# Splitting the four row scatters of each batch into two pairs, in an adaLN block with windowed attention and a routed FFN

## The chip, the cores and the metric

The kernel runs on one core of one Trainium2 chip, as one launch. The metric is the device time of that launch in microseconds, as the median of several runs. Before the change it is 313.97 us (three runs: 309.85, 313.97, 314.17).

## What is computed

Eight batches of 256 tokens, 128 wide, go through one block: a modulated layer norm, attention over windows of 64 positions (each window sees itself and the one before it) with 16 heads of 8, a gated residual, a second modulated layer norm, and an FFN with eight experts of hidden width 352, of which each token takes two. All is fp32.

```python
mod = (_silu(L0_c) @ L0_wmod).reshape(L0_c.shape[0], 6, 1, -1)
sa, ca, ga, sb, cb, gb = (mod[:, 0], mod[:, 1], mod[:, 2], mod[:, 3], mod[:, 4], mod[:, 5])
ga = (2 * (ga >= 0) - 1) * jnp.maximum(jnp.abs(ga), 0.25)
gb = (2 * (gb >= 0) - 1) * jnp.maximum(jnp.abs(gb), 0.25)
h = _layernorm(x, axis=-1) * (1 + ca) + sa
x = x + ga * _L0_attn_ref(h, L0_attn_w_qkv, L0_attn_w_out)
h = _layernorm(x, axis=-1) * (1 + cb) + sb
x = x + gb * _L0_ffn_ref(h, L0_ffn_Wg, L0_ffn_W1, L0_ffn_W3, L0_ffn_W2)

# the FFN: the two best experts of each token, weighted by a softmax of their scores
scores = xt @ Wg.T
top_vals, top_idx = jax.lax.top_k(scores, TOPK)
weights = jax.nn.softmax(top_vals, axis=-1)
h1 = jnp.einsum('td,ehd->teh', xt, W1)
h3 = jnp.einsum('td,ehd->teh', xt, W3)
expert_out = jnp.einsum('teh,edh->ted', jax.nn.silu(h1) * h3, W2)
out = jnp.sum(sel * weights[:, :, None], axis=1)
```

## The kernel before

The program is written by hand for each engine; every engine runs its own list in order, and semaphores tie them. It has two stages.

**The attention stage** takes the batches b = 0 to 7 in turn. On TensorE (PE), ScalarE (ACT) and VectorE (DVE) a batch is `period0(b)` followed by `period1(b)`. The work is pipelined over batches: `period0(b)` of PE holds the scores of the second half of batch b (`scores`, L500, 64 small matmuls in the trace), the transpose of the second norm's result of batch b-2 (`h2_transpose`, L598), the projections Q and K of batch b+1 (`project_qk`, L463 and L464), the product with V of the half before (`pv(2b-1)`, L560, 64 small matmuls), the projection V (`project_v`, L469), the transposed scores (`scores_t`, L529 to L544), the gate of batch b-2 (L607), the output's transposition of batch b-1 (`output_t`, L575) and the transposed row maxima (`neg_max_t`, L510). `period1(b)` holds the same kinds of work for the other half, with `pv(2b)`. The product with V thus ends twice in a batch and counts the semaphore `pv_done` up by one each time.

DVE reduces the scores to row maxima (`neg_max`, L993, waits for `s_done`, which the last L500 counts up). ACT copies what PE leaves in PSUM (h2 transposed, L857; Q, L819; K, L820 and L821; the output, L844; V, L825) and takes the exponentials (L832, wait for `f_done`, which the last L544 counts up).

GpSimd (POOL) has the loop of this case. For each b it multiplies Q of batch b+1 by a mask into `qm` (`mask_q`, L1352, waits for `q_copied` and `f_done`; two buffers), inverts the standard deviation of batch b-1 (`inv_std2`, L1339, waits for DVE's variance in `period1(b)`), scatters the rows of batch b-2, and scales W_out (`gate_wout`, L1345).

**The scatters** put each token's second norm, twice (once for each chosen expert), with its token number, into the DRAM tensor `routed`, at the row that the token has in its expert's region. A batch has 256 tokens in two tiles of 128 (p = 0, 1) and two choices (k = 0, 1), so four indirect DMAs of 128 rows of 516 bytes (L1363). They read `pay[e % 2]` and `row_u[e % 2]`, and count up `scattered[e % 2]` as they land. DVE refills `pay[e % 2]` for batch e+2 in `modulate_2` only after that count (L1045).

**The FFN stage** takes slots of 128 rows of one expert. SP loads a slot's rows from `routed` (L408), PE transposes them (L732), multiplies by W1 and W3 (L720, L722), transposes the gated product (L736) and multiplies by W2 (L745); POOL scatters the results into `ranked` (`store`, L1406). The first twelve slots use rows of batches 0 to 4 alone, and start once these have landed and a first table is there. Batches 6 and 7 are scattered between the first stores. At the end each token's two rows are read back, weighted and added to x.

In the scheduling of the attention stage POOL's order is fixed by its list: what stands behind a waiting instruction waits too.

## Time and profile before

| | us |
|---|---|
| median of three runs | 313.97 |
| lowest, highest | 309.85, 314.17 |
| the profiled execution | 310.88 |
| its span in the trace | 309.0 |

The profile comes from one execution, whose own time is 310.88 us; 1.9 us of it lie around the span. Of the span PE is busy 234.9 us (76%), DVE 158.3 us (51%), ACT 115.0 us (37%) and POOL 109.4 us (35%). The attention stage lasts to about 175 us, the FFN slots run to about 286 us, and the rest is the final sum. Idle time of an engine matters only where its work ends last; so the chain from engine to engine within a batch is what is to be read.

### The profile page before, as it was taken

The page shows a single profiled execution, that of the slowest core. Times are in us where ns is not written, and L with a number is a line of the kernel's source. Part 1 is how long each engine was busy: PE and PEld are TensorE (multiplying, and loading weights), DVE is VectorE, ACT ScalarE, POOL GpSimd, SP SyncE. Part 2 cuts the span into 40 slices and gives each one's busy share as a digit, 9 for nine tenths or more (in the row PEclk, how much of TensorE's full clock was granted, in tenths as well). Part 3 has the DMA queues.
Part 4 walks back from the last instruction along what each step waited for, and adds up shares of the span by engine and source line. Part 5 has one row for each costly group of instructions (what it writes and reads, how often), then busy time and mean ns, then how long its engine had stood idle before and what let it go on. Part 6 is the DMA issues. An engine that isn't in the chain of part 4 may idle for free.

```text
span 309.0 us, 9635 instructions
## 1 busy us (share of the span) xinstructions
PE 234.9 (76%) x3654; PEld 173.3 (56%) x3655; DVE 158.3 (51%) x527; ACT 115.0 (37%) x259; POOL 109.4 (35%) x119
## 2 busy tenths in 40 slices
PE   7666898987979979797875799693099999997000
PEld 3445576766657657474553566472077877876000
DVE  2656669664934637365354254463034444443393
ACT  3214455544524424354043243131034444443250
POOL 8213132235070350624205107365023443435241
PEclk9959899999998979999579589798579999999755
DMA  5599000000010000100002002112112211210551
GB/s 132 152 405 430 10 2 4 2 14 28 2 37 4 11 28 2 40 2 20 19 2 56 15 17 61 46 52 67 53 44 60 59 44 54 54 45 29 169 192 57
DMA packets 16880, 19.46 MB, mean 63 GB/s; under 512 B 2962, under 2 KB 15382, under 8 KB 16586
## 3 DMA queue, kind: packets, MB, share of 16 engines
q1 hardware_dynamic: 14170, 14.44, 14.6%
q0 software_dynamic: 2240, 4.28, 4.2%
q8 instruction: 28, 0.46, 0.6%
q10 hardware_dynamic: 432, 0.20, 0.2%
q14 instruction: 10, 0.08, 0.1%
HBM read 13.04 MB, written 6.13 MB: 62 GB/s over the span
## 4 chain that ended last, share of the span: by engine, by line
PE 48%; issue 18%; DVE 8%; ACT 7%; DMA 5%; SPq 5%; another core or an unknown queue 4%; POOL 3%; DVEq 0%; POOLq 0%; ACTq 0%
PE pair L745 7%; PE pair L720 6%; PE pair L560 6%; PE pair L722 6%; ACT pt L832 4%; PE pair L736 3%; PE pair L534 3%; PE pair L500 3%; PE pair L575 2%; DVE fin_b L1311 2%; POOL qm L1352 2%; DMA x_all<-x 2%; PE pair L469 2%; DVE nd L993 2%
## 5 line engine op out<-in xcount | busy, mean ns | idle before, releaser
L1406 POOL DMA_INDIRECT ranked<-y_sb,ix_u x36 | 35.5, 987 | 54.3 <-ACT y_sb L918 42.4
L993 DVE TENSOR_REDUCE nd<-pair 128x8 f32<-128x1024 f32 x32 | 37.6, 1218 | 32.5 <-remote 19.4
L1287 DVE TENSOR_TENSOR gated<-pair,act 128x352 f32<-128x352 f32 x36 | 18.9, 524 | 47.6 <-PE pair L722 39.6
L832 ACT ACTIVATE pt<-pair 128x1024 f32<-128x1024 f32 x32 | 32.8, 1029 | 27.3 <-PE pair L544 27.3
L1339 POOL TENSOR_TENSOR rstd<-veps,cf_sb 128x2 f32<-128x2 f32 x8 | 6.0, 747 | 84.2 <-DVE veps L1033 84.2
L1363 POOL DMA_INDIRECT routed<-pay,row_u x32 | 31.8, 994 | 9.1 <-issue 9.1
L560 PE MATMUL pair<-pt,v_lane 128*32 128x64 f32 x1024 | 27.2, 241 | 8.4 <-issue 8.0
L745 PE MATMUL pair<-we_sb,gated_t 128*128 x216 | 31.6, 285 | 1.6 <-ACT y_sb L918 1.6
L720 PE MATMUL pair<-we_sb,x_t 128*128 x72 | 29.2, 489 | 2.3 <-issue 1.8
L745 PEld LDWEIGHTS pair<-we_sb,gated_t 128*128 128x128 f32 x216 | 28.3, 199 | 2.3 <-issue 2.3
L500 PE MATMUL pair<-k_sb,qm 32*64 32x128 f32 x1024 | 25.4, 291 | 5.3 <-POOL qm L1352 1.6
L560 PEld LDWEIGHTS pair<-pt,v_lane 128*32 128x32 f32 x1024 | 20.1, 122 | 16.5 <-issue 16.5
L722 PE MATMUL pair<-we_sb,x_t 128*128 x72 | 28.3, 476 | 0.0
L1300 DVE COPY gated_t<-pair 128x384 f32<-128x384 f32 x36 | 19.8, 550 | 10.7 <-PE pair L736 6.1
L500 PEld LDWEIGHTS pair<-k_sb,qm 32*64 32x64 f32 x1024 | 18.3, 136 | 10.3 <-issue 8.8
L907 ACT ACTIVATE act<-pair 128x352 f32<-128x352 f32 x36 | 16.7, 464 | 16.7 <-PE pair L720 12.1
L918 ACT COPY y_sb<-pair 128x128 f32<-128x128 f32 x36 | 9.6, 266 | 34.3 <-issue 14.6
L732 PE MATMUL pair<-cf_sb,xt_in 128*128 128x128 f32 x36 | 10.5, 293 | 12.4 <-DMA xt_in<-routed 9.3
L722 PEld LDWEIGHTS pair<-we_sb,x_t 128*128 128x128 f32 x72 | 14.3, 198 | 8.3 <-issue 1.2
L1352 POOL TENSOR_TENSOR qm<-q_sb,quadmask 128x1024 f32<-128x1024 f32 (+1 forms) x8 | 14.3, 1786 | 12.9 <-ACT q_sb L819 12.9
L534 PE MATMUL pair<-qm,k_sb 32*128 32x256 f32 x256 | 18.7, 409 | 0.0
L736 PE MATMUL pair<-cf_sb,gated 128*128 128x128 f32 x108 | 18.4, 281 | 0.0
(167 smaller groups left out, 390.1 us busy)
## 6 DMA issues: line engine op xcount, KB each, us to landing
we_sb<-we SPq DMA_DIRECT2D x1, 4352.0 KB, 18.3
xt_in<-routed SPq DMA_DIRECT2D x36, 64.5 KB
mod_bc<-mod_rows SPq DMA_DIRECT2D x1, 2048.0 KB, 8.2
fin_y<-ranked SPq DMA_DIRECT2D x8, 256.0 KB, 4.9
out<-fin_b SPq DMA_DIRECT2D x8, 128.0 KB, 1.8
x_all<-x SPq DMA_DIRECT2D x1, 896.0 KB, 5.5
ranked<-y_sb,ix_u POOLq DMA_INDIRECT x36, 2.3
routed<-pay,row_u POOLq DMA_INDIRECT x32
```

What stands on the lines that cost most here:

```text
L500: last = mm(S_BANKS[j][64 * a:64 * a + 64, quad * P:quad * P + P], group(qm[par], j)[:, quad, c * W:c * W + W], group(k_sb[par], j)[:, c * ...
L534: mm(fv[:, :, a * W:(a + 1) * W], group(k_sb[par], j)[:, c * W:c * W + 2 * W], group(qm[par], j)[:, :, c * W:(c + 1) * W], start=False, st ...
L560: last = mm(group(Z0, j)[:, at:at + W], v_lane[par][:, c * H + 4 * j + quad, low:low + 32], pt[:, j, quad * P + a * W:quad * P + a * W + W ...
L720: mm(H1_BANK[n][:, 0:HID], x_t[n][:, :], weights((r + 1) % 4, 0, HID), start=True, stop=True).then_inc(h1_done, 1)
L722: mm(H3_BANK[n][:, 0:HID], x_t[n][:, :], weights((r + 1) % 4, HID, HID), start=True, stop=True).then_inc(h3_done, 1)
L736: last = pe.transpose(GT_BANK[r % 2][:, k * P:(k + 1) * P], gated[r % 2][:, k * P:(k + 1) * P], ident)
L745: last = mm(Y_BANK[:, 0:D], gated_t[n][:, k * P:(k + 1) * P], weights((r - 1) % 4, 2 * HID + k * D, D), start=(k == 0), stop=(k == KT - 1))
L832: act.activation(pt[:, 2 * half:2 * half + 2, :].rearrange("p j k -> p (j k)"), src[:, :], ACT.Exp).then_inc(done, 1)
L993: dve.tensor_reduce(nd[:, :, 2 * half:2 * half + 2, 0].rearrange("p s j -> p j s"), src[:, :].rearrange("p (j s k) -> p j s k", j=2, s=4), ...
L1352: pool.tensor_tensor(qm[b % 2][:, 0:quads, :], q_sb[:, :].unsqueeze(1).to_broadcast([P, quads, S]), quadmask[:, 0:quads].unsqueeze(2).to_b ...
L1363: pool.indirect_dma_start(routed[:, :], at, pay[e % 2][:, p, k, :], None).then_inc(scattered[e % 2], 16)
L1406: pool.indirect_dma_start(ranked[:, :], bass.IndirectOffsetOnAxis(ap=ix_u[q][:, 0:1], axis=0), y_sb[q][:, :], None, bounds_check=TOPK * TO ...
```

## The change

POOL issues the four scatters of a batch in two pairs. The pair of tile 0 stays where all four were, in iteration b for batch b-2. The pair of tile 1 is issued in the next iteration, ahead of `mask_q`, and waits there for `pv_done` to reach 2b, which is the end of `pv(2b-1)` in `period0(b)`. For batch 5 it stands behind the loop and waits for the last product with V. Batches 6 and 7 are as they were.

```diff
-            def scatter(e):
-                rows_chosen(e)
-                for p in range(2):
-                    scatter_tile(e, p)
-
...
             for b in range(B):
+                if b >= 3:
+                    pool.wait_ge(pv_done, 2 * b)
+                    scatter_tile(b - 3, 1)
                 if b + 1 < B:
                     mask_q(b + 1, 4)
...
                 if b >= 1:
                     inv_std2(b - 1)
                 if b >= 2:
-                    scatter(b - 2)
+                    rows_chosen(b - 2)
+                    scatter_tile(b - 2, 0)
                 gate_wout(b)
+            pool.wait_ge(pv_done, G)
+            scatter_tile(B - 3, 1)
             inv_std2(B - 1)
```

On POOL, in the loop, at the place of the scatters of batch 0 (`pay0`) and batch 1 (`pay1`); `qm0` and `qm1` are the two mask buffers:

```order
-L1363 DMA routed<-pay0,row_u0 17536x129 x4
+L1363 DMA routed<-pay0,row_u0 17536x129 x2
 L1345 TENSOR_TENSOR wout_g<-wout_sb,mod_bc 128x128
+L1363 DMA routed<-pay0,row_u0 17536x129 x2
 L1352 TENSOR_TENSOR qm0<-q_sb,quadmask 128x1024
 L1339 TENSOR_TENSOR rstd2<-veps2,cf_sb 128x2
-L1363 DMA routed<-pay1,row_u1 17536x129 x4
+L1363 DMA routed<-pay1,row_u1 17536x129 x2
 L1345 TENSOR_TENSOR wout_g<-wout_sb,mod_bc 128x128
+L1363 DMA routed<-pay1,row_u1 17536x129 x2
 L1352 TENSOR_TENSOR qm1<-q_sb,quadmask 128x1024
```

Of each four, two now stand behind `gate_wout` and before the next mask, so that the mask has a wait for `pv_done` and two scatters ahead of it.

The same piece of POOL's list after the change, with what each instruction waits for:

```order
L1339 TENSOR_TENSOR rstd<-veps,cf_sb 128x2 [waits var2_ready]
L1363 DMA routed<-pay,row_u 17536x129 [waits pay_ready,rows_ready]
L1363 DMA routed<-pay,row_u 17536x129
L1345 TENSOR_TENSOR wout_g<-wout_sb,mod_bc 128x128 [waits y_done]
L1363 DMA routed<-pay,row_u 17536x129 [waits pv_done]
L1363 DMA routed<-pay,row_u 17536x129
L1352 TENSOR_TENSOR qm<-q_sb,quadmask 128x1024 [waits f_done,q_copied]
```

The wait for `pv_done` stands at the first scatter of the second pair alone.

On PE, where nothing moves, the list around that `pv` in `period0`:

```order
L500 MATMUL pair<-k_sb,qm 64x128 x32
L598 MATMUL pair<-cf_sb,pay 128x128 [waits h2_ready,exp_z]
L598 MATMUL pair<-cf_sb,pay 128x128
L463 MATMUL pair<-h_t,wqkv_sb 128x256 [waits ht_ready]
L464 MATMUL pair<-h_t,wqkv_sb 128x256
L560 MATMUL pair<-pt,v_lane 32x64 [waits v_copied,exp_z]
L560 MATMUL pair<-pt,v_lane 32x64 x31
L469 MATMUL pair<-wqkv_sb,h_t 128x128 [waits negt_ready]
L469 MATMUL pair<-wqkv_sb,h_t 128x128 x3
L529 MATMUL pair<-negt,cb_sb 128x512 [waits exp_z,o_copied,exp_x,h2t_copied,max_x,negt_ready]
```

The second pair is released when the last L560 has ended, so beside L469 and what follows it; the first pair is released by DVE and ACT, about when L500 runs. (An fp32 matmul stands once here and twice in the trace.)

## Rows read from the trace of the kernel before

**Rows 1.** Busy time by batch: start:end length, busy (instructions), PEclk, DMA share, GB/s.

```profile
50.49:65.65 15.16, 14.15 (x407) 10.93 (x407) 11.95 (x38) 8.60 (x17) 3.05 (x3) 1.00 0.02 4
65.65:84.19 18.54, 15.79 (x407) 11.64 (x407) 11.05 (x38) 8.56 (x17) 7.16 (x7) 1.00 0.05 17
84.19:104.34 20.15, 17.51 (x407) 12.88 (x407) 10.62 (x38) 8.39 (x17) 7.12 (x7) 0.92 0.05 16
104.34:124.52 20.18, 17.58 (x407) 12.90 (x406) 10.61 (x38) 8.36 (x17) 7.12 (x7) 0.92 0.05 16
124.52:142.54 18.02, 15.71 (x389) 11.41 (x389) 10.78 (x36) 7.77 (x16) 7.12 (x7) 1.00 0.06 18
142.54:164.77 22.23, 17.76 (x294) 11.99 (x294) 10.12 (x47) 6.21 (x11) 5.23 (x7) 0.69 0.05 15
164.77:186.13 21.36, 15.62 (x125) 10.72 (x122) 7.77 (x39) 7.71 (x16) 5.22 (x6) 0.76 0.13 32
```

**Rows 2.** Timeline of POOL, batch 2's scatters: start, us, engine line [idle before].

```profile
104.34 0.76 POOL L1339 TENSOR_TENSOR rstd<-veps,cf_sb 128x2 f32<-128x2 f32 x1 [10.86 <-DVE veps L1033]
105.30 1.12 POOL L1363 DMA_INDIRECT routed<-pay,row_u  x1 [0.20 <-issue]
...
109.25 0.96 POOL L1363 DMA_INDIRECT routed<-pay,row_u  x1 [0.30 <-issue]
...
111.72 1.89 POOL L1352 TENSOR_TENSOR qm<-q_sb,quadmask 128x1024 f32<-128x1024 f32 x1 [1.02 <-ACT q_sb L819]
```

**Rows 3.** Timeline of PE, DVE and ACT beside and behind those scatters.

```profile
107.62 0.72 PE L560 MATMUL pair<-pt,v_lane 128*32 128x64 f32 x10
...
108.74 0.34 PE L560 MATMUL pair<-pt,v_lane 128*32 128x64 f32 x6 [0.40 <-issue]
...
110.95 2.36 DVE L993 TENSOR_REDUCE nd<-pair 128x8 f32<-128x1024 f32 x2 [5.20 <-remote]
110.96 0.81 PE L560 MATMUL pair<-pt,v_lane 128*32 128x64 f32 x39 [0.44 <-issue]
110.99 0.37 ACT L857 COPY h_t<-pair 128x256 f32<-128x256 f32 x1 [4.93 <-remote]
...
111.70 1.98 PE L469 MATMUL pair<-wqkv_sb,h_t 128*128 128x128 f32 x8
...
116.16 1.02 ACT L832 ACTIVATE pt<-pair 128x1024 f32<-128x1024 f32 x1 [1.86 <-PE pair L544]
```

**Rows 4.** The same timeline a stage earlier, in a batch without scatters.

```profile
51.98 2.34 DVE L993 TENSOR_REDUCE nd<-pair 128x8 f32<-128x1024 f32 x2
...
54.44 1.16 PE L469 MATMUL pair<-wqkv_sb,h_t 128*128 128x128 f32 x8
...
57.29 1.02 ACT L832 ACTIVATE pt<-pair 128x1024 f32<-128x1024 f32 x1 [1.07 <-PE pair L544]
...
59.14 1.21 PE L500 MATMUL pair<-k_sb,qm 32*64 32x128 f32 x64
```

**Rows 5.** Timeline of PE and ACT beside batch 5's scatters (165.72 to 170.63).

```profile
167.41 1.30 PE L560 MATMUL pair<-pt,v_lane 128*32 128x64 f32 x45
167.52 0.37 ACT L857 COPY h_t<-pair 128x256 f32<-128x256 f32 x1 [0.70 <-PE pair L598]
```

**Rows 6.** Timeline: last of seven indirect DMAs in a row, and PE behind it.

```profile
211.80 0.99 POOL L1406 DMA_INDIRECT ranked<-y_sb,ix_u  x1 [0.31 <-issue]
...
212.86 0.85 PE L720 MATMUL pair<-we_sb,x_t 128*128 x2 [1.82 <-issue]
```

**Rows 7.** Stretches of 2 us behind those scatters: PE busy (instructions), PEclk, DMA share.

```profile
110.00:112.00 2.00, 1.34 (x45) 0.96 0.10 33
112.00:114.00 2.00, 2.00 (x12) 0.50 0.04 8
```

**Rows 8.** Timeline of PE and ACT in batch 7's first half, behind batch 4's scatters.

```profile
150.39 1.94 PE L560 MATMUL pair<-pt,v_lane 128*32 128x64 f32 x64
...
156.08 1.02 ACT L832 ACTIVATE pt<-pair 128x1024 f32<-128x1024 f32 x1 [3.31 <-PE pair L544]
```

## The prediction, made before the changed kernel ran

> **What bounds the kernel now.** I read the busy time by batch first. Six stretches, each from one `inv_std2` (L1339) to the next, differ in one thing: the first, 50.49 to 65.65, has no scatter and takes 15.16 us; the next four have four scatters each and take 18.54, 20.15, 20.18 and 18.02 us, with (but for the last) the same 407 matmuls. POOL's busy time grows by 4 us in them, yet POOL is busy only 7 of 18 to 20 us, so POOL isn't the bound. Two more stretches, 142.54 and 164.77, take 22.23 and 21.36 us [rows 1]. What do the scatters do to the others?
>
> The timeline answers. POOL issues the scatters of batch 2 from 105.30 to 109.25 + 0.96 = 110.21 [rows 2]. Beside them, PE starts `pv` at 107.62, does 10 of its 64 matmuls, and then goes on in small groups: 6 at 108.74, two more groups like it, and the last 39 at once from 110.96. DVE's `neg_max`, which waits for nothing but the end of L500, is idle for 5.20 us and starts at 110.95; ACT's copy L857, which waits for the transpose on PE, is idle for 4.93 us and starts at 110.99 [rows 3]. Three engines come free together, 0.74 us behind the last scatter. So while scatters are generated, PE's signals reach others late, and PE itself stops once some tens of its instructions are out. Batch 5's scatters show the second part alone: PE comes to them idle, ACT gets its signal after 0.70 us, 45 of the 64 matmuls go out at full speed, and only then does PE stop [rows 5]. I call this state the slow phase. It ends with the burst: also behind a burst of seven in the FFN stage, whose last ends at 211.80 + 0.99 = 212.79, and PE goes on at 212.86 [rows 6]. So it ends 0.1 to 0.7 us behind the last indirect DMA.
>
> The chain of a batch runs through it: `pv`, then L469, then the transposed scores, then the exponentials (L832, "pt"). Without scatters L469 starts at 54.44, 3.95 us into the stretch, and pt at 57.29, 6.80 in [rows 4]. With them L469 starts at 111.70, 7.36 in, and pt at 116.16, 11.82 in [rows 3]. From pt to the next L1339 both take the same: 65.65 - 57.29 = 8.36 and 124.52 - 116.16 = 8.36. All that a stretch loses, it loses before pt.
>
> A part of the loss is the clock. In the stretches of 20.15 and 20.18 us the granted clock is 0.92 in the mean, in those of 18.54 and 18.02 it is 1.00 [rows 1]: behind the slow phase, in which PE does little, it falls to 0.50, the lower level (1.2 GHz), for about 3 us [rows 7]. L469 then takes 1.98 us instead of 1.16 [rows 3, 4]. The price is 20.15 - 18.54 = 1.6 us.
>
> **The change, part by part.**
>
> *First pair stays.* A scatter costs POOL 0.96 + 0.30 = 1.26 us [rows 2]. With two fewer, the burst ends 2.52 us earlier, at 107.69, and the slow phase at 108.43 instead of 110.95. DVE and ACT start 2.5 us earlier. PE has 54 of the 64 matmuls left; 39 took until L469 starts 0.74 us later [rows 3], so 54 take 1.0: L469 at 109.4, 5.1 us into the stretch, and the wait for `pv_done` is over at the same time.
>
> *Second pair.* POOL starts it 0.20 later and needs 1.12 + 0.30 + 0.96 = 2.38 us [rows 2]: 109.6 to 112.0. This makes a second slow phase, until 112.7. PE does L469 and the transposed scores in it, 32 matmuls (8, 4, 16, 4) before the last group, against the 128 of L500 and `pv` in the old one. By the row of 45 matmuls [rows 5] PE has room for that many without a stop, so PE is not stopped; but the signal for the exponentials is behind in the queue and comes with the end of the phase. By PE's own pace pt would start 57.29 - 54.44 = 2.85 us behind L469 [rows 4], at 112.25; by the slow phase at 112.7 to 112.8. I take 112.8, that is 8.4 us into the stretch. The bounds: 7.95 (PE's own pace), and 9.2 if the phase ends 0.7 us later.
>
> *A stretch* is then 8.4 + 8.36 = 16.8 us. Against 18.54 and 18.02 I take 1.7 us each (18.02 has 18 matmuls fewer, so its new length is shorter too), against 20.15 and 20.18 3.4 each, because the poor stretch of PE falls from over 5 us to about 2.5 and I expect the clock to hold. Together 10.2 us. If the clock falls as before, 3.2 less.
>
> *Stretch 142.54.* Here `pv` starts at 150.39, takes 1.94 us at half clock, and pt starts at 156.08 [rows 8]. Its start moves 2.5 earlier, to 147.9; its end is 149.0 to 149.8 by the clock; plus 0.2 + 2.38 + 0.74 gives pt at 152.3 to 153.1. That is 3.0 to 3.8 earlier; I take 3.5.
>
> *Stretch 164.77.* 45 matmuls go out by 168.7 [rows 5], beside which the first pair would end at 168.1. The remaining 19 took four groups of five, some 0.74 us apart (110.96 less two such steps in rows 3), 2.9 us; now 0.4. The second pair (batch 5, behind the loop) lies beside the gate and `output_t`, 12 matmuls. The clock may return earlier. I take 3.0 (bounds 1.5 and 4.5).
>
> *The wait and what it holds.* Behind the waiting scatter stand the mask (L1352), `inv_std2` and the first pair of the next batch. The mask ran from 111.72 for 1.89 us [rows 2]; it now runs from about 112.1 to 114.0. L500 of the next half needs it, 59.14 - 57.29 = 1.85 us behind pt [rows 4], so at 114.6, with 0.6 us to spare. The cover is thin: if pt starts at 112.25, L500 is due at 114.1 and little is left. I put 0.2 us a stretch on it, 1.0 in all. `inv_std2` isn't due before the end of the stretch. DVE refills `pay` only at the start of the next stretch, over 8 us behind the second pair. SP's first loads need batch 4's second pair, issued before pt of batch 7's first half; the table that they also need is written in `period1(7)`, later. All these cost nothing.
>
> *Sum.* 10.2 + 3.5 + 3.0 - 1.0 = 15.7 us. The profiled execution takes 310.88, so 295.2. The median of the three runs lies 3.1 above that execution and its lowest run 1.0 below; I add half of 3.1, since part of such scatter between runs may be the clock behind these phases: 296.7.
>
> **The rivals.**
>
> *The second burst gives most of it back (16 in 100).* The phase ends 0.7 us later than I took, and the clock falls as in rows 7. A stretch is 9.2 + 8.36 + 1.6 = 19.2, against a mean of (18.54 + 20.15 + 20.18 + 18.02) / 4 = 19.2: four stretches gain nothing, the last two some 4: about 307 to 309. For it: two phases have two beginnings and two ends. Against: the second lies beside a quarter of the matmuls.
>
> *Nothing changes (7 in 100).* The late signals have another cause, and the scatters merely lie beside it. Then it stays at 311 to 314. Against it: six bursts with the same picture, and a stretch without any [rows 1, 4].
> The Trainium skill's page "SBUF — State Buffer", section "Who interferes with whom", speaks for this rival: only VectorE and GpSimd share a port pair, and TensorE and ScalarE never wait on anyone. By it a scatter being generated couldn't hold PE, and the change would be worth 0 instead of 15.7 us. Rows 3 disagree, with PE stopped and ACT 4.93 us idle, though the cause need not be a port of SBUF.
>
> *Slower: the slow phase has a fixed length (5 in 100).* It lasted 110.95 - 105.30 = 5.65 us. If two scatters make as long a phase as four, L469 stays at 7.36 us in, the second phase ends at 7.36 + 0.2 + 5.65 = 13.2, and pt with it, against 11.8 (half clock) and 18.54 - 8.36 = 10.2 (full clock). Two stretches lose 1.4, two 3.0, the last two perhaps 1 each: 310.9 + 10.8 = 322. It decides once a pair's phase is longer than some 4.5 us. Against it: the ends of rows 3 and 6 follow the last DMA, after four and after seven.
>
> **How the numbers follow.** The forecast has 72 in 100, with its own range 289 (PE's own pace, upper bounds of the last two) to 303 (the clock falls, lower bounds). With half of the first rival the range reaches 306. This kernel's measurement can tell about 2%, 6.3 us of 313.97, from no change. All of the forecast and half of the first rival lie under 307.7: faster 0.80. The other half and "nothing changes": 0.15. Slower: 0.05.
>
> **What would show it.** In the new trace each of the four stretches should take about 17 us with a clock of 1.00; DVE's L993 should start 0 to 0.8 us behind the second scatter's end, its wait down from 5.2 to about 2.7; L469 should start about 5 us in; the second pair should start 0.2 us behind `pv`, and pt 0.7 behind its end. The mask should end before L500 is due, with a PE wait for POOL under 0.3. Wrong would be: `pv` still in small groups behind the pair's end; a pt later than 9.2 in; a clock of 0.5 behind either pair; a PE wait for `qm` of a microsecond.

## The result, and the profile after

The changed kernel takes 291.53 us in the median of 4 runs (289.18 to 293.05), the kernel before 312.34 on the same chip (4 runs, 309.85 to 314.17). The ratio is 0.933, with a 95% interval of 0.923 to 0.944: faster by 6.7%. The forecast was 296.7 (289 to 306). The profiled execution takes 289.18 us, 21.7 less than that of before; its granted clock is 0.894 in the mean, against 0.874. Here and below a ratio leaves out runs at a lower clock that took over 1.5% longer than the fastest of their kernel, while medians and ranges count every run.

The busy time by batch, from one `inv_std2` (L1339) to the next; columns as in rows 1 (start:end, length, then busy time and instructions of PE, PEld, DVE, ACT and POOL, granted clock, DMA share, GB/s):

```profile
50.53:65.70 15.17, 14.15 (x407) 10.95 (x407) 11.96 (x38) 8.59 (x17) 3.05 (x3) 1.00 0.02 4
65.70:81.62 15.92, 14.79 (x407) 11.22 (x407) 10.50 (x38) 8.38 (x17) 7.21 (x8) 1.00 0.06 20
81.62:97.47 15.85, 14.93 (x407) 11.21 (x406) 10.51 (x38) 8.38 (x17) 7.17 (x8) 1.00 0.06 20
97.47:113.34 15.87, 14.93 (x407) 11.20 (x405) 10.49 (x38) 8.37 (x17) 7.17 (x8) 1.00 0.06 20
113.34:128.71 15.37, 14.86 (x389) 10.98 (x388) 9.98 (x36) 7.61 (x16) 7.16 (x7) 1.00 0.07 21
128.71:146.95 18.24, 14.10 (x294) 10.00 (x294) 10.02 (x47) 7.16 (x12) 5.26 (x6) 0.81 0.06 18
146.95:164.40 17.45, 13.91 (x121) 9.77 (x122) 7.77 (x39) 6.92 (x16) 5.24 (x7) 0.80 0.15 39
```

The stretch without scatters is what it was (15.17 us). The six with scatters are 2.6, 4.3, 4.3, 2.6, 4.0 and 3.9 us shorter than in [rows 1], 21.8 together: the whole difference of the two executions lies here, and nothing is given back in the FFN stage behind it. POOL is as busy as before, 7.2 us in a stretch. The clock is 1.00 in the four middle stretches, where two of them had 0.92.

What a stretch looks like now. This is the timeline of PE, its weight loads (PEld), DVE, ACT and POOL in the stretch from 97.47; columns: start, us, engine, line, operation, out<-in, and in brackets the idle time before it:

```profile
99.85 0.96 POOL L1363 DMA_INDIRECT routed<-pay,row_u  x1 [0.30 <-issue]
...
100.75 1.45 PE L560 MATMUL pair<-pt,v_lane 128*32 128x64 f32 x64
...
101.14 0.89 PEld L560 LDWEIGHTS pair<-pt,v_lane 128*32 128x32 f32 x57 [0.25 <-issue]
101.32 2.36 DVE L993 TENSOR_REDUCE nd<-pair 128x8 f32<-128x1024 f32 x2 [2.44 <-remote]
101.36 0.37 ACT L857 COPY h_t<-pair 128x256 f32<-128x256 f32 x1 [2.18 <-remote]
...
102.12 1.16 PE L469 MATMUL pair<-wqkv_sb,h_t 128*128 128x128 f32 x8
...
102.47 1.01 POOL L1363 DMA_INDIRECT routed<-pay,row_u  x1 [1.18 <-PE pair L560]
...
103.79 0.96 POOL L1363 DMA_INDIRECT routed<-pay,row_u  x1 [0.30 <-issue]
...
104.63 0.29 PE L544 MATMUL pair<-cb_sb,late 32*32 32x256 bf16 x4
...
104.77 1.90 POOL L1352 TENSOR_TENSOR qm<-q_sb,quadmask 128x1024 f32<-128x1024 f32 x1
...
105.32 1.09 PE L575 MATMUL pair<-perm_o,o_sb 128*128 128x72 f32 x8
105.32 1.02 ACT L832 ACTIVATE pt<-pair 128x1024 f32<-128x1024 f32 x1 [1.42 <-PE pair L544]
...
106.45 0.36 DVE L1007 RECIPROCAL rden<-pair 128x32 f32<-128x32 f32 x1 [2.31 <-PE pair L575]
...
106.82 1.21 PE L500 MATMUL pair<-k_sb,qm 32*64 32x128 f32 x64
```

The first pair ends at 99.85 + 0.96 = 100.81. DVE and ACT start 0.51 and 0.55 us later, both out of a wait put down to "remote": the mark of the slow phase is still there, but the wait is 2.44 us instead of 5.20 [rows 3]. `pv` is no longer cut into small groups: its 64 matmuls are one row of 1.45 us, and only their weight loads pause once, for 0.25 us after the seventh. (Without scatters `pv` takes 1.10 us.) The second pair starts 0.27 us behind them and ends at 104.75, and the exponentials (`pt`) start at 105.32, 7.85 us into the stretch; before it was 11.82 [rows 3], without scatters 6.80 [rows 4]. The mask ends at 106.67 and L500 starts at 106.82, 9.35 us in (8.65 without scatters [rows 4]).

One subtraction sorts the rest. L469 starts 4.65 us in, against 3.95 without scatters [rows 4]: 0.70 late. The stretch is 15.87 us long, against 15.17: 0.70 as well. So in this stretch all that the scatters still cost is the first pair's; the second costs nothing.

### The profile page after: what moved, and what is told of

It is laid out like the page before. It is cut to its first block, busy times and chain, and to the rows that moved or that the text cites. A ratio compares the mean times of both kernels' runs of the same rounds, so it can differ in the third digit from the quotient of the medians.

```text
span 287.3 us, 9635 instructions
## 1 busy us (share of the span) xinstructions
PE 223.6 (78%) x3654; PEld 165.8 (58%) x3655; DVE 157.2 (55%) x527; ACT 114.8 (40%) x259; POOL 109.4 (38%) x119
## 4 chain that ended last, share of the span: by engine, by line
PE 51%; issue 16%; DVE 10%; POOL 8%; ACT 5%; DMA 4%; another core or an unknown queue 2%; ACTq 1%; SPq 1%; POOLq 0%; DVEq 0%
PE pair L745 8%; PE pair L720 8%; PE pair L722 7%; PE pair L560 4%; PE pair L736 4%; PE pair L500 3%; ACT pt L832 3%; POOL routed L1363 3%; POOL qm L1352 3%; PE pair L534 3%; DVE fin_b L1311 2%; PE pair L575 2%; PE pair L732 2%; DVE nd L993 2%
## 5 line engine op out<-in xcount | busy, mean ns | idle before, releaser
L993 DVE TENSOR_REDUCE nd<-pair 128x8 f32<-128x1024 f32 x32 | 37.7, 1220 | 19.1 <-remote 9.8
L1363 POOL DMA_INDIRECT routed<-pay,row_u x32 | 32.1, 1003 | 16.8 <-PE pair L560 9.5
L720 PE MATMUL pair<-we_sb,x_t 128*128 x72 | 30.3, 505 | 3.7 <-ACT x_t L912 3.7
L745 PE MATMUL pair<-we_sb,gated_t 128*128 x216 | 31.0, 280 | 1.7 <-ACT y_sb L918 1.7
L722 PE MATMUL pair<-we_sb,x_t 128*128 x72 | 29.2, 488 | 0.0
L745 PEld LDWEIGHTS pair<-we_sb,gated_t 128*128 128x128 f32 x216 | 27.7, 196 | 2.3 <-issue 2.3
L1339 POOL TENSOR_TENSOR rstd<-veps,cf_sb 128x2 f32<-128x2 f32 x8 | 6.0, 744 | 58.2 <-DVE veps L1033 58.2
L500 PE MATMUL pair<-k_sb,qm 32*64 32x128 f32 x1024 | 24.0, 292 | 3.6 <-DVE qm L1168 1.5
L500 PEld LDWEIGHTS pair<-k_sb,qm 32*64 32x64 f32 x1024 | 17.8, 137 | 7.8 <-issue 6.1
L918 ACT COPY y_sb<-pair 128x128 f32<-128x128 f32 x36 | 9.6, 266 | 31.1 <-issue 15.9
L560 PE MATMUL pair<-pt,v_lane 128*32 128x64 f32 x1024 | 20.7, 232 | 0.3
L560 PEld LDWEIGHTS pair<-pt,v_lane 128*32 128x32 f32 x1024 | 17.2, 117 | 5.1 <-issue 5.0
L912 ACT COPY x_t<-pair 128x128 f32<-128x128 f32 x36 | 9.6, 266 | 21.8 <-PE pair L732 17.0
L534 PE MATMUL pair<-qm,k_sb 32*128 32x256 f32 x256 | 17.2, 381 | 0.0
```

The lines of the kernel that those rows point to most:

```text
L500: last = mm(S_BANKS[j][64 * a:64 * a + 64, quad * P:quad * P + P], group(qm[par], j)[:, quad, c * W:c * W + W], group(k_sb[par], j)[:, c * ...
L534: mm(fv[:, :, a * W:(a + 1) * W], group(k_sb[par], j)[:, c * W:c * W + 2 * W], group(qm[par], j)[:, :, c * W:(c + 1) * W], start=False, st ...
L560: last = mm(group(Z0, j)[:, at:at + W], v_lane[par][:, c * H + 4 * j + quad, low:low + 32], pt[:, j, quad * P + a * W:quad * P + a * W + W ...
L720: mm(H1_BANK[n][:, 0:HID], x_t[n][:, :], weights((r + 1) % 4, 0, HID), start=True, stop=True).then_inc(h1_done, 1)
L722: mm(H3_BANK[n][:, 0:HID], x_t[n][:, :], weights((r + 1) % 4, HID, HID), start=True, stop=True).then_inc(h3_done, 1)
L745: last = mm(Y_BANK[:, 0:D], gated_t[n][:, k * P:(k + 1) * P], weights((r - 1) % 4, 2 * HID + k * D, D), start=(k == 0), stop=(k == KT - 1))
```

## Experiments

All times are medians; where a ratio has an interval, it is against the kernel before on the same chip. "Stretches" are the six lengths that follow the stretch without scatters, in the order of the profile. Each diff shows the part that matters, with ` ...` where lines are left out. Where lines are added ahead of them, a kernel's line numbers are a little higher than those of the kernel before; the text says which is which.

### The split without the hold

```diff
             for b in range(B):
                 if b >= 3:
-                    pool.wait_ge(pv_done, 2 * b)
                     scatter_tile(b - 3, 1)
 ...
-            pool.wait_ge(pv_done, G)
             scatter_tile(B - 3, 1)
```

> The four scatters stay split in two pairs in POOL's list, but the second pair no longer waits for the end of the product with V; only gate_wout (0.47 us) lies between the pairs. Theory 'place' (the loss comes from how many PE instructions stand beside the scatters while they are generated): POOL runs one burst of some 5.4 us again, beside L500 and pv, DVE's L993 waits about 5 us, and each of the four full stretches from one inv_std2 to the next takes 18 to 20.5 us instead of 15.9; the time is that of the kernel before, 308 to 316 us. Rival 'split' (two short bursts are milder than one long one, wherever they are): the gap ends the slow phase, stretches of 16 to 17 us, time 290 to 298 us.

Measured: 312.55 us (10 runs, 309.57 to 314.59), ratio 0.995 [0.991, 1.000]. Stretches 18.65, 20.13, 20.22, 19.67, 22.35 and 21.38. One stretch of it, by busy time as above:

```profile
84.68:104.81 20.13, 17.26 (x407) 12.84 (x407) 11.53 (x38) 8.57 (x17) 7.19 (x8) 0.92 0.05 16
```

POOL's timeline in it shows that only `gate_wout` (L1345) now stands between the two pairs:

```profile
87.07 0.96 POOL L1363 DMA_INDIRECT routed<-pay,row_u  x1 [0.30 <-issue]
88.05 0.47 POOL L1345 TENSOR_TENSOR wout_g<-wout_sb,mod_bc 128x128 f32<-128x128 f32 x1
88.68 1.01 POOL L1363 DMA_INDIRECT routed<-pay,row_u  x1 [0.17 <-issue]
```

What DVE and PE do beside and behind them:

```profile
89.33 2.36 DVE L993 TENSOR_REDUCE nd<-pair 128x8 f32<-128x1024 f32 x2 [3.23 <-remote]
...
91.56 1.07 PE L560 MATMUL pair<-pt,v_lane 128*32 128x64 f32 x27 [0.42 <-issue]
```

The stretch has the old length, but it isn't the old picture. I had expected DVE's L993 to wait for 5 us; it waits for 3.23, and in the four full stretches for 2.57, 3.23, 3.23 and 2.52, about 2 less than with four in a row (4.54, 5.21, 5.20 and 4.48). With the gap of 0.65 us DVE's signal comes through 1.30 us behind the first pair's end and with the third scatter still running. PE doesn't come free: `pv` goes on in small groups, and its last 27 matmuls start at 91.56, 0.60 us behind the last scatter's end (90.96). So what makes the stretch long is that PE is stopped at `pv`; the early signal to DVE gains nothing by itself.

The medians, 312.55 and 312.89, differ by 0.1%, and the ratio leaves at most 1%: the program order alone can't be told from no change. The gain is in the wait for `pv_done`, that is, in where the second pair runs.

### All four held

```diff
                 if b >= 3:
                     pool.wait_ge(pv_done, 2 * b)
+                    rows_chosen(b - 3)
+                    scatter_tile(b - 3, 0)
                     scatter_tile(b - 3, 1)
 ...
-                if b >= 2:
-                    rows_chosen(b - 2)
-                    scatter_tile(b - 2, 0)
                 gate_wout(b)
             pool.wait_ge(pv_done, G)
+            rows_chosen(B - 3)
+            scatter_tile(B - 3, 0)
             scatter_tile(B - 3, 1)
```

> All four scatters of a batch are held until pv in period0 has ended, none is left beside L500. Theory 'place': the first half of the stretch runs as in one without scatters, L469 starts about 4.0 us in; the burst then lies from 4.2 to 9.1 us in, the signal for the exponentials comes with its end, pt at about 9.7 instead of 7.85, so a stretch takes 9.7 + 8.36 = 18.1 us; the time is about 299 to 303 us. Rival 'only dense matmuls matter' (behind pv the scatters cost nothing, since PE has few instructions there): pt at 7 to 7.3, stretches of 15.3 to 15.7 us, if not for the mask, which ends 11 us in, where L500 is due 9 in; with that wait about 17, time 293 to 296 us and a PE wait for qm of 1 to 2 us.

Measured: 304.7 us (4 runs, 303.34 to 305.9), ratio 0.973 [0.968, 0.978]. Stretches 17.74, 19.28, 19.81, 19.07, 17.25 and 19.82. The second of them:

```profile
81.98:101.26 19.28, 16.07 (x396) 12.13 (x392) 10.79 (x38) 8.56 (x16) 7.04 (x8) 0.91 0.05 17
```

Its timeline (ACT, DVE, PE):

```profile
91.52 1.02 ACT L832 ACTIVATE pt<-pair 128x1024 f32<-128x1024 f32 x1 [2.21 <-PE pair L544]
...
93.75 0.36 DVE L1007 RECIPROCAL rden<-pair 128x32 f32<-128x32 f32 x1 [6.25 <-remote]
...
94.83 1.20 PE L500 MATMUL pair<-k_sb,qm 32*64 32x128 f32 x64 [1.91 <-POOL qm L1352]
```

`pt` starts 91.52 - 81.98 = 9.54 us in, as expected (9.7). The total was missed by both expectations: the median lies 1.7 us above the range of the theory (299 to 303), and the rival had the PE wait for `qm` right (1 to 2 us) but not the times. Two things make this stretch longer than the 18.1 expected. DVE's L1007, which waits for L575, starts only 0.99 us behind the burst's end (92.76), 11.77 us into the stretch; without scatters it is 58.77 - 50.49 = 8.28. From L1007 to the next L1339 it takes 6.9 us where nothing comes between (shown under "Second pair" below), which makes 18.65. The other 0.6 us come with the mask, for which PE waits 1.91 us, and with the clock (0.91 in this stretch, 0.83 in the third). The place behind `pv` is better than the old one even for four, but a burst there has limits of its own: the next signals that are due, and POOL's next product.

### No scatters at all, and the same bytes by direct DMAs

The batches' scatters (batches 0 to 5) are left out of the kernel before; `routed` is filled once with the padding row by SP so that the FFN stage has what to read. This fill moves everything behind it 8.4 us later, so only lengths are compared.

```diff
                 if b >= 1:
                     inv_std2(b - 1)
-                if b >= 2:
-                    scatter(b - 2)
                 gate_wout(b)
```

> The kernel before without the scatters of batches 0 to 5 (their rows never reach the experts; routed and ranked are filled with padding rows by SP after the weights instead, so that the slots have something to read). Theory 'the scatters are the whole difference': each of the four full stretches takes 15.2 us as the one without scatters does, PEclk 1.00, and the last two lose 5 us or more each; span 278 to 284 us. Rival 'the scatters merely lie beside it': stretches stay at 18 to 20 us, span near 309.

Measured: 293.27 us, one run (the kernel before beside it: 313.91, one run). Stretches 15.16, 15.17, 15.23, 14.62, 14.08 and 19.72. By busy time:

```profile
74.08:89.24 15.16, 14.12 (x407) 10.90 (x405) 11.94 (x38) 8.56 (x17) 3.05 (x4) 1.00 0.01 3
...
148.34:168.06 19.72, 16.08 (x121) 11.50 (x122) 7.96 (x39) 6.92 (x16) 1.15 (x3) 0.65 0.09 21
```

From the first to the last row of these six it is 93.98 us, against 120.48 before and 98.70 after. By that the scatters cost 26.5 us and 4.7 are left, but the last stretch spoils the sum: at a clock of 0.65 it takes 19.72 us without any scatter near, more than the changed kernel's 17.45. That can't come from slow phases; it comes back below. The first five alone take 74.26 us here, 99.12 before and 81.25 after: the scatters cost 24.9 there, and 7.0 of it are left. The span, 291.4 us, is over the 278 to 284 expected, by less than the fill's 8.4 us; and the last stretch lost 1.6 us where 5 or more had been expected.

In the next kernel each batch's four blocks of `pay` go to a scratch area by four direct DMAs of the same size, issued by SP, with their completion counted; the rows aren't scattered.

```diff
 ...
+                for p in range(2):
+                    for k in range(TOPK):
+                        at = (4 * e + 2 * p + k) * P
+                        sp.dma_start(aside_rows[at:at + P, :], pay[e % 2][:, p, k, :]).then_inc(direct[e % 2], 16)
```

> The kernel before with POOL's four scatters of each of batches 0 to 5 replaced by four direct DMAs of the same 128 x 516 bytes from SP's queue into another DRAM tensor (the rows never reach the experts; padding rows are filled in instead). The same bytes leave in rows of the same size at the same point of the stretch. Theory 'generation on POOL': no slow phase, DVE's L993 starts as without scatters, stretches of 15.2 to 15.5 us, span 278 to 284. Rival 'traffic': the rows on their way to DRAM, or their completion signals, hold PE's signals; stretches of 17 to 20 us, span over 295.

Measured: 291.4 us, one run. Stretches 15.17, 15.15, 15.23, 14.62, 14.08 and 19.58; the second one:

```profile
87.99:103.14 15.15, 14.11 (x407) 10.90 (x407) 11.94 (x38) 8.56 (x17) 3.05 (x3) 1.00 0.08 21
```

The same to 0.14 us as with no scatters, though the DMA share rises from 0.01 to 0.08. So the same bytes in direct DMAs of SP, with their completion signals, make no slow phase. (The span, 289.5 us, is again over the range, with a fill and a last stretch as in the kernel without scatters.)

### The same four DMAs from POOL, direct instead of indirect

Again the blocks go to the scratch area and the rows aren't scattered; the rows are written one behind the other.

```diff
                 for p in range(2):
                     for k in range(TOPK):
-                        at = bass.IndirectOffsetOnAxis(ap=row_u[e % 2][:, 2 * p + k:2 * p + k + 1], axis=0)
-                        pool.indirect_dma_start(routed[:, :], at, pay[e % 2][:, p, k, :], None).then_inc(scattered[e % 2], 16)
+                        at = (4 * e + 2 * p + k) * P
+                        pool.dma_start(aside_rows[at:at + P, :], pay[e % 2][:, p, k, :]).then_inc(scattered[e % 2], 16)
```

> The kernel before with the four scatters of each of batches 0 to 5 replaced by four direct DMAs of the same 128 x 516 bytes from POOL's own queue into another DRAM tensor (the rows never reach the experts; padding rows are filled in instead). In the profile such a DMA takes POOL about 0.7 us instead of 0.96. Theory 'generation on POOL, whatever its kind': a shorter burst (about 3.5 us with the gaps), a slow phase of 4 to 4.5 us, stretches of 16.5 to 18.5 us, span 288 to 300. Rival 'only the indirect form does it': stretches of 15.2 us, span 278 to 284.

Measured: 287.21 us, one run. Stretches 15.08, 15.08, 15.14, 14.50, 14.61 and 15.54. By busy time:

```profile
87.69:102.77 15.08, 14.20 (x407) 10.94 (x405) 11.83 (x38) 8.56 (x17) 5.28 (x8) 1.00 0.07 21
...
147.02:162.56 15.54, 11.12 (x125) 8.14 (x122) 7.79 (x39) 7.60 (x16) 3.39 (x7) 1.00 0.20 44
```

And POOL and DVE in the timeline (L1004 is what is L993 in the kernel before):

```profile
88.40 2.20 POOL L1381 DMA_DIRECT2D aside_rows<-pay  x4
...
89.10 2.36 DVE L1004 TENSOR_REDUCE nd<-pair 128x8 f32<-128x1024 f32 x2
```

This struck down my theory that any DMA that POOL issues makes the slow phase: it expected 16.5 to 18.5 us a stretch. POOL works 2.20 us on four direct ones, at the place and from the buffers of the old scatters, and PE doesn't notice. Nor is it that 2.20 us are too short to be felt: a pair of indirect ones takes POOL 2.38 us at this place and makes DVE wait for 2.44, while here DVE starts L1004 with no wait, beside POOL's work. It is the indirect form that does it. What the targets add, rows spread over `routed` against rows in order, wasn't tested by itself.

### Half the rows in each scatter

The scatters stay where they were, but each writes 64 rows instead of 128; the other half of the routed rows is left out.

```diff
-                        at = bass.IndirectOffsetOnAxis(ap=row_u[e % 2][:, 2 * p + k:2 * p + k + 1], axis=0)
-                        pool.indirect_dma_start(routed[:, :], at, pay[e % 2][:, p, k, :], None).then_inc(scattered[e % 2], 16)
+                        at = bass.IndirectOffsetOnAxis(ap=row_u[e % 2][0:W, 2 * p + k:2 * p + k + 1], axis=0)
+                        pool.indirect_dma_start(routed[:, :], at, pay[e % 2][0:W, p, k, :], None).then_inc(scattered[e % 2], 16)
```

> The kernel before with each of the four scatters of batches 0 to 5 cut to its first 64 rows (the other rows never reach the experts; padding rows are filled in by SP after the weights). Theory 'the slow phase is the making of the indirect descriptors, row by row': a scatter takes POOL 0.5 to 0.7 us instead of 0.96, the burst about 3.5 us instead of 4.9, and the stretches are 16 to 17.5 us. Rival 'a fixed cost of the indirect form': the same 0.96 us and stretches of 18 to 20 us. A third outcome: the same time on POOL but a shorter or no slow phase, which would tie the slow phase to the rows and not to POOL's busy time.

Measured: 317.73 us, one run (before: 310.81), with a start that the fill moves later. Stretches 18.54, 20.21, 20.12, 19.67, 20.87 and 21.36, in all 120.8 us against 120.5 before. By busy time:

```profile
89.79:110.00 20.21, 17.17 (x407) 12.79 (x407) 10.63 (x38) 8.47 (x17) 6.83 (x7) 0.92 0.04 9
```

And from the timeline of the next stretch:

```profile
114.70 0.90 POOL L1381 DMA_INDIRECT routed<-pay,row_u  x1 [0.30 <-issue]
...
116.64 0.37 ACT L867 COPY h_t<-pair 128x256 f32<-128x256 f32 x1 [4.92 <-remote]
```

(L867 is what is L857 in the kernel before, and L1381 are the scatters.) Half the rows (9 GB/s instead of 16) save POOL 0.06 us of 0.96 and PE nothing; ACT idles 4.92 us as before. The theory that the price is paid row by row fell, and the fixed cost held: between 64 and 128 rows the price goes with the number of indirect DMAs, not with rows or bytes. The burst ends at 114.70 + 0.90 = 115.60 and ACT comes free 1.04 us later, where it was 0.78 before [rows 2, 3].

### The mask ahead of the second pair

```diff
             for b in range(B):
+                if b + 1 < B:
+                    mask_q(b + 1, 4)
                 if b >= 3:
                     pool.wait_ge(pv_done, 2 * b)
                     scatter_tile(b - 3, 1)
-                if b + 1 < B:
-                    mask_q(b + 1, 4)
```

> As the changed kernel, but POOL writes the mask for the next batch ahead of the wait and the second pair, so the pair starts about 6.7 us into the stretch instead of 5.0. Theory 'signals are queued': the pair then lies beside the transposed scores' last matmuls and their signal, which comes with the end of the pair, 9.1 + 0.5 = 9.6 us in, and beside the next L500; pt at 9.0 to 9.6, stretches of 17.3 to 18 us, time 297 to 301 us. Rival 'the end of pv alone matters': any place behind pv is as good, and the mask is no longer near PE's need: stretches of 15.5 to 15.9, time 288 to 292 us.

Measured: 295.83 us (4 runs, 294.3 to 298.14), ratio 0.942 [0.936, 0.947]. Stretches 16.51, 16.56, 16.52, 16.07, 20.80 and 20.03. Busy time and timeline of the second:

```profile
82.81:99.37 16.56, 15.01 (x407) 11.32 (x406) 10.63 (x38) 8.37 (x17) 7.14 (x8) 1.00 0.06 19
```

```profile
90.74 1.09 PE L575 MATMUL pair<-perm_o,o_sb 128*128 128x72 f32 x8
90.89 0.96 POOL L1363 DMA_INDIRECT routed<-pay,row_u  x1 [0.30 <-issue]
90.94 1.02 ACT L832 ACTIVATE pt<-pair 128x1024 f32<-128x1024 f32 x1 [1.62 <-PE pair L544]
...
92.47 0.36 DVE L1007 RECIPROCAL rden<-pair 128x32 f32<-128x32 f32 x1 [2.78 <-PE pair L575]
```

A stretch takes 16.5 us instead of 15.9: neither the 17.3 to 18 of the theory that the pair's end rules `pt`, nor no cost at all. `pt` starts 8.13 us in, 0.91 ahead of the pair's end (91.85), so that signal came through. But the one behind it did not: DVE's `rden` (L1007) waits for L575 and starts 1.73 us behind that line's start and 0.62 behind the pair's end, where in the changed kernel it starts 1.13 behind L575 (105.32 to 106.45). 0.60 us late here, 0.6 us longer the stretch. From L1007 to the end of the stretch it is 6.90 us, as everywhere. So a pair costs by the signal that is due when it ends; moving it 1.8 us later (6.8 us in, not 5.0) made it meet another one. The time, 295.83 us, is between the two expectations as well, but only 2.6 us of it are these four stretches: the fifth takes 20.80 us at a clock of 0.61 and the sixth 20.03 at 0.73, though no mask is moved in them. The changed kernel has 18.24 and 17.45 there, and 17.72 and 19.56 in a second profile. Why isn't known.

### Each pair behind a `pv`

```diff
                 if b >= 3:
                     pool.wait_ge(pv_done, 2 * b)
-                    scatter_tile(b - 3, 1)
+                    rows_chosen(b - 3)
+                    scatter_tile(b - 3, 0)
                 if b + 1 < B:
                     mask_q(b + 1, 4)
+                if b >= 3:
+                    pool.wait_ge(pv_done, 2 * b + 1)
+                    scatter_tile(b - 3, 1)
```

(The pair of tile 0 at its old place is gone, and behind the loop the last batch's four follow the last `pv`.)

> Both pairs are held: the first until pv in period0 has ended, the second until pv in period1 has ended, each with a burst of its own behind a pv; nothing is left beside L500. Theory 'place': the first pair ends 6.6 us in, pt at 7.15 instead of 7.85 (0.7 us less a stretch), and the second pair delays the second exponentials by about as much (phase end 14.7 us in, instead of 14.0): stretches of 15.7 to 16.1, time 288 to 293 us, as the changed kernel. Rival 'what is left of the loss lies all in the first pair beside L500': stretches of 15.2 to 15.4 us, time 284 to 288 us. A third outcome: the rows land too late for DVE's refill of pay (L1046), which then waits, and a stretch takes 16.3 or more.

Measured: 289.41 us (4 runs, 288.01 to 290.99), ratio 0.924 [0.918, 0.931]. Stretches 15.17, 16.19, 15.84, 15.34, 15.80 and 19.27. By busy time:

```profile
65.75:80.92 15.17, 14.10 (x391) 10.85 (x390) 10.59 (x38) 7.77 (x16) 7.11 (x7) 1.00 0.07 21
```

From its timeline:

```profile
72.99 1.03 ACT L832 ACTIVATE pt<-pair 128x1024 f32<-128x1024 f32 x1 [1.51 <-PE pair L544]
...
80.55 1.02 ACT L832 ACTIVATE pt<-pair 128x1024 f32<-128x1024 f32 x1 [2.52 <-PE pair L544]
```

With one pair behind the first `pv` (70.10 to 72.48) and nothing at the old place, `pt` starts 7.24 us in, 0.44 later than without scatters, and the stretch still takes 15.17 us, as without: a pair in this place costs nothing. The second pair, which POOL issues from 77.59 to 79.87, holds up the second exponentials in the same way (idle 2.52 us), and its price shows in the next stretch, 15.8 us or so. In the middle stretches two pairs behind two `pv` cost as much as the changed kernel's two places. The gain is in the stretch from 128 (15.80 against 18.24): there the first pair at its old place still caught L500.

One thing could have spoiled the comparison: the pair behind the second `pv` lands late, and DVE waits for it before it refills `pay` (waits: total us, count, longest):

```profile
DVE pay L1046 <- DMA routed<-pay,row_u: 2.8, 2, 2.3
```

The two waits lie in the last two stretches, before the refills at 130.99 (2.27 us) and 145.08 (0.56).

A third buffer of `pay`, and of `row_u` and the count that goes with it, takes that wait away; in that kernel batch 5's scatters are placed as in the changed kernel.

```diff
-        pay = [sb(f"pay{i}", [P, 2, TOPK, PAY]) for i in range(2)]
+        pay = [sb(f"pay{i}", [P, 2, TOPK, PAY]) for i in range(3)]
 ...
```

> As the run with both pairs behind a pv, with a third buffer for pay and row_u, so that DVE's refill no longer waits for the second pair to land, and with batch 5's pairs as in the changed kernel. Theory 'signals': what that run still loses (0.7 us a stretch) is the second pair's slow phase in front of the second exponentials; the third buffer changes it by 0.2 us at most, stretches of 15.6 to 15.9 us, time 286 to 290. Rival 'landing': the refill's wait for the rows to land was the loss; stretches of 15.2 us, time 283 to 286.

Measured: 287.39 us (4 runs, 286.54 to 288.32), ratio 0.928 [0.922, 0.933]. Stretches 15.18, 15.86, 15.79, 15.28, 14.48 and 19.48.

The first four stretches don't move by more than 0.33 us, as the theory had it: in them the late signal is the cost, not the landing. The stretch from 128 becomes 1.3 us shorter, though this kernel differs there in the buffers and in batch 5's place at once, so that gain isn't divided between them.

### One, two and one

```diff
                 if b >= 3:
                     pool.wait_ge(pv_done, 2 * b)
-                    scatter_tile(b - 3, 1)
+                    scatter_tile(b - 3, 0, (1,))
+                    scatter_tile(b - 3, 1, (0,))
                 if b + 1 < B:
                     mask_q(b + 1, 4)
+                if b >= 3:
+                    pool.wait_ge(pv_done, 2 * b + 1)
+                    scatter_tile(b - 3, 1, (1,))
 ...
-                    scatter_tile(b - 2, 0)
+                    scatter_tile(b - 2, 0, (0,))
```

> The four scatters of a batch go out as one, two and one: the first where all four were (behind inv_std2, beside L500), the next two behind pv of period0 as the changed kernel's second pair, the last behind pv of period1. Batch 5's last three stand behind the last pv. Theory 'place and length': a single scatter's slow phase (1.0 us and 0.5) ends before anything on the chain needs a signal. Beside L500 it releases L993 about 2.6 us into the stretch, where L529 needs its result only at 5.1; behind the second pv it ends 13.3 us in, before f_done at 13.7. So the 0.7 us a stretch that the changed kernel still loses goes: stretches of 15.2 to 15.4 us instead of 15.87, time 282 to 286 us, 2 to 2.5% under the changed kernel's. Rival 'each burst costs its own beginning and end': three bursts cost more than two, stretches of 16.2 or more, time 291 to 295.

Measured: 287.84 us (4 runs, 283.53 to 288.92), ratio 0.921 [0.910, 0.932]. Stretches 15.71, 15.31, 15.52, 14.90, 14.92 and 19.58. DVE in the timeline of the third of them, which starts at 96.16:

```profile
98.62 2.36 DVE L993 TENSOR_REDUCE nd<-pair 128x8 f32<-128x1024 f32 x2 [1.06 <-PE pair L500]
```

With a single scatter at the old place DVE's wait is 1.06 us, where a pair makes 2.44 and four made 5.20, and L993 starts 2.46 us into the stretch. The first four stretches are 0.1 to 0.6 us above those without scatters, the fifth 0.8. So the theory was right that a single scatter is the mildest and the rival (16.2 or more) fell, but 15.2 to 15.4 us wasn't reached throughout, and the time is above the 282 to 286 expected; the last stretch, 19.58 us, is as long as in the two kernels beside it.

The changed kernel ran once more in the same comparison:

> The changed kernel once more, beside the other orders on the same chip: 289 to 293 us, four stretches of 15.4 to 15.9 us.

Measured: 292.71 us (4 runs, 291.71 to 293.33), ratio 0.944 [0.939, 0.950]. Stretches 15.91, 15.87, 15.85, 15.35, 17.72 and 19.56; the last by busy time:

```profile
146.17:165.73 19.56, 15.38 (x133) 10.94 (x130) 7.78 (x39) 7.71 (x16) 5.25 (x7) 0.74 0.13 35
```

The middle four repeat to 0.02 us; the last one took 17.45 us at a clock of 0.80 in the first profile and takes 19.56 at 0.74 here. On this chip "one, two and one" is 292.71 - 287.84 = 4.9 us below the changed kernel, 1.7%, and the kernel with three buffers 5.3 us. No run of either reaches into those of the changed kernel beside them (at most 288.92 against at least 291.71). Between the two of them the times don't decide. Against the kernel before these three comparisons are less firm: its seven runs on this chip go from 308.59 to 368.00 us.

## Why the prediction was right, point by point

The direction and the mechanism held, the time came 5 us under the forecast. The working was 15.7 us of saving on the profiled execution; it is 21.7. In the four middle stretches 13.9 us were saved, more than even the better bound of the working allows (10.2 and four times 0.45, 12.0): the range held because it was wide, not because each term was.

**What bounds the kernel: right, and now shown.** The reading was that scatters being issued on POOL hold up PE and its signals. Without scatters the stretches with 18.0 to 20.2 us take 14.6 to 15.2; with the same bytes from SP too. The reading lacked one word, "indirect": direct DMAs on POOL do nothing of the kind. And it took the late signals and the stop of PE for one thing: without the hold DVE's signal came 2 us earlier and the stretch stayed as long, so at the old place the stop of PE is what costs. "Nothing changes" is out with that. That rival had the Trainium skill's page "SBUF — State Buffer", section "Who interferes with whom", behind it, by which TensorE and ScalarE never wait on anyone. The runs disagree for whatever it is that indirect DMAs do: ACT is idle for 4.93 us ahead of its copy L857 [rows 3], and for 0.27 us in the kernel whose POOL sends the same bytes from the same buffers by direct DMAs. They don't say that it is a port of SBUF.

**The end of the slow phase: right.** DVE and ACT start 0.51 and 0.55 us behind the first pair's end (0 to 0.8 was named), DVE's wait is 2.44 us (about 2.7).

**First pair, a term sized too small.** I had PE free again 0.74 us behind the pair's end, with 54 matmuls left that take 1.0 us, and L469 at 5.1 us in. The 1.0 us was right: 57 weight loads are left, and from them (101.14) to L469 (102.12) it is 0.98. What was mis-sized is the end of the phase for PE: 101.14 - 100.81 = 0.33 us behind the pair's end, not 0.74. `pv` has hardly begun to be held by then, and L469 starts 102.12 - 97.47 = 4.65 us in, 0.45 better.

**Second pair, the other one.** I took `pt` at 8.4 (bounds 7.95 and 9.2); it is 7.85. From L469 to `pt` it takes 3.20 us, against 2.85 without scatters [rows 4]: the pair makes the signal only 0.35 us late. That signal comes 0.57 us behind the pair's end, as the text had it (0.7 to 0.8). The step that failed is the next one: "a stretch is then 8.4 + 8.36", all that is lost before `pt` is lost for good. From `pt` to the next L1339 it takes 113.34 - 105.32 = 8.02 us, 0.34 less than the 8.36 carried over. What the end of the stretch hangs on is not `pt` but DVE's L1007, which waits for L575 and not for the exponentials. These are its rows in the kernel before, in the stretch without scatters and in one with four:

```profile
56.95 0.29 PE L544 MATMUL pair<-cb_sb,late 32*32 32x256 bf16 x4
...
58.77 0.36 DVE L1007 RECIPROCAL rden<-pair 128x32 f32<-128x32 f32 x1 [2.62 <-PE pair L575]
...
117.64 0.36 DVE L1007 RECIPROCAL rden<-pair 128x32 f32<-128x32 f32 x1 [3.75 <-PE pair L575]
```

From L1007 to the next L1339 it takes 6.88 us (58.77 to 65.65), 6.88 (117.64 to 124.52) and 6.89 in the changed kernel (106.45 to 113.34), whether `pt` is late or not. L500 too starts 2.19 us behind L544 in both (104.63 to 106.82; 56.95 to 59.14 without scatters). The 8.36 was the same in both rows of before because `pt` started 0.34 us behind L544 in each, which a pair beside it changes. By my working the part from L469 to the end of the stretch is 16.8 - 5.1 = 11.7 us; it is 15.87 - 4.65 = 11.22, and 15.16 - 3.95 = 11.21 without scatters [rows 1, 4]. A delay of `pt` by 0.35 us is swallowed whole. Together the four stretches save 13.9 us for a forecast of 10.2.

**The clock in the four stretches: right.** It stays at 1.00.

**The last two stretches: nearly right, in part by luck.** Saved are 4.0 (forecast 3.5) and 3.9 (forecast 3.0, bounds 1.5 and 4.5). In the second profile of the changed kernel it is 4.5 and 1.8, so how close the two sizes came is a matter of the execution; the clock is 0.80 in the last stretch of one and 0.74 in that of the other. In the first of the two stretches the first pair still catches L500 and then the clock falls, as this timeline of PE and ACT in the changed kernel shows:

```profile
129.64 0.99 PE L500 MATMUL pair<-k_sb,qm 32*64 32x128 f32 x33
130.91 2.58 PE L500 MATMUL pair<-k_sb,qm 32*64 32x128 f32 x31 [0.28 <-issue]
...
134.05 1.94 PE L560 MATMUL pair<-pt,v_lane 128*32 128x64 f32 x64
...
139.06 1.02 ACT L832 ACTIVATE pt<-pair 128x1024 f32<-128x1024 f32 x1 [2.64 <-PE pair L544]
```

33 matmuls go out at speed, the other 31 take 2.58 us, and `pv` behind them takes 1.94, as in [rows 8]. So "`pv` starts 2.5 earlier at half clock" held as it was put (5.34 us in, against 7.85), and `pt` is 3.2 us earlier (10.35 us in, against 13.54), inside the 3.0 to 3.8.

**The mask: right on the mechanism, priced too high.** I put 1.0 us on it. It ends 0.15 us before L500 starts, L500 starts 2.19 us behind L544 as without scatters, and PE has no wait for `qm`. The cover is as thin as the text said: with two scatters more (all four held) PE waits 1.91 us.

**The sum.** 13.9 + 4.0 + 3.9 is 21.8, against 10.2 + 3.5 + 3.0 - 1.0: of the 6.1 us missed, 3.7 lie in the two sizes above (0.45 and 0.48 in each of four stretches), 1.4 in the last stretches, 1.0 in the mask. The 1.5 us added for the median was 2.35. "The second burst gives it back" and "a fixed length" fell: one scatter makes 1.06 us of DVE's wait, two 2.44, four 5.20, and without scatters there is none.

**What stays open.** Which part of an indirect DMA on POOL does it, and by what path it reaches PE, wasn't separated; that 64 rows cost nearly what 128 do speaks for something fixed in each. And why the clock falls in the last stretch (0.65 with no scatters, 1.00 with direct DMAs from POOL, 0.80 and 0.74 in two profiles of the changed kernel) isn't explained; it is worth up to 4 us (19.72 against 15.54), so single profiles can't rank kernels that differ by less there. For the same reason the 1.7% of "one, two and one" rests on its runs alone, whose spread is 5.4 us, and not on stretches of one profile.

## What to carry to other kernels

When several engines come out of waits put down to "remote" at one moment, and PE runs in small groups just before, look for what POOL did until then; indirect DMAs cost other engines more than POOL's own time. Place them where PE has few matmuls to issue and no signal that another engine needs next, in bursts of one or two, and look at what POOL owes next, since that cover is thin. A short gap in a burst isn't enough: it let DVE's signal through here and still kept PE in small groups. Where the rows are known beforehand, the direct form costs nothing here, from SP or from POOL.

## What the runs showed of the hardware

- An indirect DMA of 64 rows takes POOL 0.90 us, one of 128 rows 0.96, each with 0.30 us behind it; four direct ones of 128 rows take 2.20 together. Only the indirect ones slow PE and its signals: a batch's stretch of 15.2 us becomes 18.5 to 20.2 with four in a row, 15.9 with two and two, 15.3 to 15.7 with one, two and one.
- With four in a row the late signals come up to 1.0 us behind the burst's end (0.74 in rows 3, 0.99 in the kernel with all four held, 1.04 with half the rows), behind a pair 0.5 to 0.6 us.
- The stretch's cost isn't proportional to the scatters: beside a pair `pv` starts in full and takes 1.45 us, beside four it goes out in groups of about five, 0.74 us apart. Behind the stop the granted clock fell to 0.50 [rows 7] in two of the four full stretches of the kernel before, which are 1.6 us longer.
- The clock in the last stretch differs between executions of one kernel (0.80 and 0.74, 17.45 and 19.56 us), with each stretch ahead of it the same within 0.6 us.
